# The last tile's feed-forward in a two-layer decoder kernel: h quantised by pieces and turned by TensorE inside the down product of the tile ahead

## The reference

```
def fp4_quant_dequant(x):            # blocks of 16
    scale = max(max|block| / 6, 1e-12)
    idx = searchsorted(MID, |block / scale|)
    return GRID[idx] * sign(block) * scale
def fp4_linear(x, w):  return einsum('bsk,nk->bsn', quant(x), quant(w))
h = silu(fp4_linear(x, w_gate)) * fp4_linear(x, w_up)
x = layernorm(x + fp4_linear(h, w_down))
```

## Time and profile before

| what | us |
|---|---|
| median of 3 runs | 2803.29 (2802.55 to 2804.59) |
| the profiled execution | 2801.17 |
| its span | 2799.6 |
| busy: TensorE matmul / VectorE / GpSimd / ScalarE | 2630.1 / 1907.7 / 865.4 / 808.7 |
| mean granted clock of TensorE | 0.978 of 2.4 GHz |

### The profile page before, as it was taken

How to read it: one execution, slowest core, us unless ns; L and a number is a source line. 1 busy time by engine, 2 the same in 40 slices (tenths; PEclk the granted TensorE clock), 3 DMA queues, 4 the chain that set the end, 5 groups by cost and what they waited for, 6 DMA issues and landing times. The chain is left out here.

```text
span 2799.6 us, 36866 instructions
## 1 busy us (share of the span) xinstructions
PE 2630.1 (94%) x13006; PEld 1586.6 (57%) x13006; DVE 1907.7 (68%) x3304; ACT 808.7 (29%) x1193; POOL 865.4 (31%) x902
## 2 busy tenths in 40 slices
PE   7999988999998889999998679999999999999996
PEld 3444534555555444444444346777777777777774
DVE  3688403666667336666678658888888888888884
ACT  1111312333332246666668511111111111111110
POOL 1232103554554346666667501111111111111000
PEclk9999989999999999999999989999999999999998
DMA  5344130000000133333335501111111111111111
GB/s 161 118 164 173 49 112 14 1 1 1 1 1 1 54 104 93 87 95 92 99 101 147 159 27 41 43 44 43 43 43 43 43 44 43 43 44 44 40 38 34
DMA packets 219395, 176.91 MB, mean 63 GB/s; under 512 B 38319, under 2 KB 184111, under 8 KB 218190
## 3 DMA queue, kind: packets, MB, share of 16 engines
q1 hardware_dynamic: 182230, 147.85, 17.6%
q10 hardware_dynamic: 36984, 26.71, 3.5%
HBM read 90.51 MB, written 52.43 MB: 51 GB/s over the span
## 5 line engine op out<-in xcount | busy, mean ns | idle before, releaser
L2016 PE MATMUL bank<-tiles,tl_XQT 128*128 128x512 f32 (+1 forms) x768 | 331.8, 575 | 7.6 <-DMA tl_XQT<-tl_QB 4.9
L2031 PE MATMUL bank<-tiles,tl_HT 128*128 128x512 f32 x704 | 316.3, 605 | 19.7 <-DMA tl_HT<-tl_tmp 19.7
L2021 PE MATMUL bank<-tiles,tl_XQT 128*128 128x512 f32 (+1 forms) x768 | 318.0, 557 | 0.0
L2031 PEld LDWEIGHTS bank<-tiles,tl_HT 128*128 128x128 f32 x704 | 225.2, 324 | 95.3 <-issue 28.0
L2016 PEld LDWEIGHTS bank<-tiles,tl_XQT 128*128 128x128 f32 x768 | 232.5, 310 | 74.0 <-issue 16.4
L2021 PEld LDWEIGHTS bank<-tiles,tl_XQT 128*128 128x128 f32 x768 | 236.7, 308 | 65.6 <-issue 0.2
L1376 POOL TENSOR_SCALAR_AFFINE_SELECT tiles<-tiles 128x512 f32<-128x512 f32 x256 | 179.5, 704 | 202.6 <-ACT tiles L1595 187.2
L1969 POOL TENSOR_TENSOR tl_rs<-tl_ve,mhalf 128x1 f32<-128x1 f32 x32 | 17.6, 549 | 593.0 <-DVE tl_ve L2124 593.0
L2065 ACT ACTIVATE tl_HQ<-bank 128x512 f32<-128x512 f32 (+1 forms) x96 | 53.9, 562 | 427.7 <-PE bank L2016 406.3
L1702 DVE SCALAR_TENSOR_TENSOR tiles<-tiles,bank 128x1024 f32<-128x1024 f32 (+1 forms) x128 | 141.7, 1148 | 25.2 <-PE bank L1475 25.2
L1381 POOL TENSOR_SCALAR_AFFINE_SELECT tiles<-tiles 128x512 f32<-128x512 f32 x224 | 152.6, 681 | 0.0
(11 more groups left out here) (279 smaller groups left out, 4961.1 us busy)
## 6 DMA issues: line engine op xcount, KB each, us to landing
tl_HT<-tl_tmp SPq DMA_DIRECT2D x256, 44.0 KB, 1.9
tl_HT<-tl_tmp ACTq DMA_DIRECT2D x256, 44.0 KB, 2.0
fp_weights<-space_quant ACTq DMA_DIRECT2D x33, 256.0 KB, 2.2
X<-in_x SPq DMA_DIRECT2D x8, 1024.0 KB, 12.0
v<-tiles SPq DMA_DIRECT2D x32, 256.0 KB, 2.4
unit_g<-tiles SPq DMA_DIRECT2D x32, 256.0 KB, 2.4
unit_gT<-tiles SPq DMA_DIRECT2D x32, 256.0 KB, 2.8
la_GN<-unit_g SPq DMA_DIRECT2D x128, 64.0 KB, 2.0
```

What stands on the lines that cost most here:

```text
L2016: mm = e.matmul(bank[(2 * q) % 3][:, 0:w], chunk(XQT[n % 2], c), WgT[q][:, :, c, :], start=(c == 0), stop=(c == C - 1))
L2021: mm = e.matmul(bank[(2 * q + 1) % 3][:, 0:w], chunk(XQT[n % 2], c), WuT[q][:, :, c, :], start=(c == 0), stop=(c == C - 1))
L2031: mm = e.matmul(bank[DOWN][:, :], chunk(HT, q), WdT[:, q, :], start=(q == 0), stop=(q == IC - 1))
```

## The change

For the last tile alone (`LT`, tile 31) the h path is a different one; the other 31 tiles keep theirs (`by_blocks`).

- VectorE: `last_h(q)` quantises piece q by itself, all nine steps, with `XB` in place of `tmp`. `last_h(0)` stands in slot 31 behind `h_turned(30)` and ahead of `product(31, 1)`, `last_h(1)` behind that product, `last_h(2)` behind `product(31, 2)`, where `h_divide` stood. The multiplication with the scales is done by quarters of the row (one behind piece 0, one behind piece 1, two behind piece 2) and writes into the other `HQ` buffer (`HL`) in such an order that each chunk of the down product is a run of 128 columns.
- TensorE: in `down(30)`, ahead of its ninth matmul, `last_turned` waits for all products and all four multiplications, and makes 11 transposes of 128 x 128 into banks 0, 1 and 2.
- ScalarE: `last_copied`, in slot 31 behind the last SiLU, copies the three banks into `tmp` (`HLT`), which the DMAs of tile 30 have left by then.
- TensorE: `last_down` in slot 32 multiplies from there, into bank 4, each group of four chunks behind its copy. It does not wait for `out_sum(30)`.
- Gone for tile 31: `h_divide`, `h_rounders`, `h_rounded`, `h_scaled`, `h_turned` over the whole width, and the 16 DMAs.

```
--- before.py
+++ after.py
@@ -1881,6 +1881,7 @@
         s_g, s_sg, s_u, s_h, s_hs, s_hq = (sem(n) for n in ("gate_mm", "silu", "up_mm", "h", "h_step", "hq"))
         s_ht, s_hd, s_d, s_a6, s_t6, s_m6, s_v6, s_r6, s_x6, s_out = (sem(n) for n in (
             "hq_turned", "hqT", "down_mm", "sum6", "stats6", "mean6", "var6", "rstd6", "x6", "stored"))
+        s_ls, s_lq, s_lt, s_lc = (sem(n) for n in ("last_h_step", "last_hq", "last_hqT_mm", "last_hqT"))
         XT, PT, SM = sb("XT", [P, C, P]), sb("PT", [P, P]), sb("SM", [P, HM])
         mx, sm, rc = (sb(n, [P, H]) for n in ("mx", "sm", "rc"))
         st4, mv4, ve4, rs4 = sb("st4", [P, 6]), [sb(f"mv4{p}", [P, 2]) for p in range(2)], sb("ve4", [P, 1]), sb("rs4", [P, 1])
@@ -1904,6 +1905,10 @@
         x_tile = lambda n: k.x_tile(n % B, n // B)
         rows = lambda n: slice(HM * (n % 2), HM * (n % 2) + HM)
         there = lambda n: 0 <= n < NT
+
+        LT = NT - 1
+        by_blocks = lambda n: 0 <= n < LT
+        HL, HLT = HQ[NT % 2], tmp
         SLOTS = range(-3, NT + 3)
 
         def blocks_moved(e, token_rows, src, dst, done):
@@ -1941,7 +1946,7 @@
                         n = s - 2
                         e.wait_ge(s_x6.sem, s_x6.at(n + 1))
                         e.dma_start(k.out[n % B, (n // B) * P:(n // B + 1) * P, :], x_tile(n)).then_inc(s_out.sem, 16)
-                    if there(s - 1):
+                    if by_blocks(s - 1):
                         h_moved(e, s - 1, (0, 1))
                     if there(s + 1):
                         xq_moved(e, s + 1, (0, 1))
@@ -2028,7 +2033,24 @@
                     e.wait_ge(s_a6.sem, s_a6.at(n))
                     e.wait_ge(s_hd.sem, s_hd.at(256 * (n + 1)))
                     for q in range(IC):
+                        if n == LT - 1 and q == IC - 3:
+                            last_turned()
                         mm = e.matmul(bank[DOWN][:, :], chunk(HT, q), WdT[:, q, :], start=(q == 0), stop=(q == IC - 1))
+                    mm.then_inc(s_d.sem, 1)
+
+                def last_turned():
+                    e.wait_ge(s_h.sem, s_h.at(NP * NT))
+                    e.wait_ge(s_lq.sem, s_lq.at(4))
+                    for q in range(IC):
+                        mm = e.transpose(bank[q // C][:, q % C * P:(q % C + 1) * P], HL[:, q * P:(q + 1) * P], k.ident[:, :])
+                        if q % C == C - 1 or q == IC - 1:
+                            mm.then_inc(s_lt.sem, 1)
+
+                def last_down():
+                    e.wait_ge(s_a5.sem, s_a5.at(NT))
+                    for q in range(IC):
+                        e.wait_ge(s_lc.sem, s_lc.at(q // C + 1))
+                        mm = e.matmul(bank[VOUT][:, :], HLT[:, q * P:(q + 1) * P], WdT[:, q, :], start=(q == 0), stop=(q == IC - 1))
                     mm.then_inc(s_d.sem, 1)
 
                 for s in SLOTS:
@@ -2046,8 +2068,10 @@
                         gate_and_up(s, 2)
                     if there(s + 2):
                         transpose_weights(s + 2)
-                    if there(s - 1):
+                    if by_blocks(s - 1):
                         down(s - 1)
+                    if s - 1 == LT:
+                        last_down()
                     if there(s + 2):
                         attend(s + 2)
 
@@ -2072,6 +2096,12 @@
                     e.wait_ge(s_pm.sem, s_pm.at(n + 1))
                     e.wait_ge(s_v.sem, s_v.at(n))
                     e.activation(PT[rows(n), :], bank[WEIGHTS][rows(n), 0:P], ACT.Copy).then_inc(s_pc.sem, 1)
+
+                def last_copied():
+                    e.wait_ge(s_hd.sem, s_hd.at(256 * LT))
+                    for n, (x, w) in enumerate(PIECES):
+                        e.wait_ge(s_lt.sem, s_lt.at(n + 1))
+                        e.activation(HLT[:, x:x + w], bank[n][:, 0:w], ACT.Copy).then_inc(s_lc.sem, 1)
 
                 for s in SLOTS:
                     if there(s + 2):
@@ -2082,10 +2112,12 @@
                         exp(s + 2)
                     if there(s):
                         silu(s, 1)
-                    if there(s - 1):
+                    if by_blocks(s - 1):
                         h_moved(e, s - 1, (2, 3))
                     if there(s):
                         silu(s, 2)
+                    if s == LT:
+                        last_copied()
                     if there(s + 2):
                         copy_weights(s + 2)
                     if there(s + 1):
@@ -2096,7 +2128,7 @@
                 def out_sum(n):
                     y = x_tile(n)
                     e.wait_ge(s_d.sem, s_d.at(n + 1))
-                    e.tensor_tensor(y, bank[DOWN][:, :], y, ALU.add).then_inc(s_a6.sem, 1)
+                    e.tensor_tensor(y, bank[DOWN if by_blocks(n) else VOUT][:, :], y, ALU.add).then_inc(s_a6.sem, 1)
                     e.wait_ge(s_a6.sem, s_a6.at(n + 1))
                     e.bn_stats(st6[:, :], y).then_inc(s_t6.sem, 1)
                     e.wait_ge(s_t6.sem, s_t6.at(n + 1))
@@ -2236,16 +2268,50 @@
                     e.wait_ge(s_hq.sem, s_hq.at(n + 1))
                     e.transpose(turned(tmp[:, :]), HQ[n % 2][:, :]).then_inc(s_ht.sem, 1)
 
+                def last_h(q):
+                    (x, w), n, at = PIECES[q], LT, QUANT * q
+                    part = slice(x // BLK, (x + w) // BLK)
+                    y, t, c, r = HQ[n % 2][:, x:x + w], XB[:, 0:w], sc[n % 2][:, part], rs[:, part]
+                    e.wait_ge(s_h.sem, s_h.at(NP * n + q + 1))
+                    e.wait_ge(s_hs.sem, s_hs.at(QUANT * n))
+                    e.tensor_reduce(am[:, part], blocks(y), AX.X, ALU.max, apply_absolute_value=True).then_inc(s_ls.sem, 1)
+                    e.wait_ge(s_ls.sem, s_ls.at(at + 1))
+                    e.tensor_scalar(c, am[:, part], 1.0 / 6.0, 1e-12, ALU.mult, ALU.max).then_inc(s_ls.sem, 1)
+                    e.wait_ge(s_ls.sem, s_ls.at(at + 2))
+                    e.reciprocal(r, c).then_inc(s_ls.sem, 1)
+                    e.wait_ge(s_ls.sem, s_ls.at(at + 3))
+                    e.tensor_scalar(r, r, 1.0 - 2.0 ** -23, None, ALU.mult).then_inc(s_ls.sem, 1)
+                    e.wait_ge(s_ls.sem, s_ls.at(at + 4))
+                    e.tensor_tensor(blocks(y), blocks(y), spread(r), ALU.mult).then_inc(s_ls.sem, 1)
+                    e.wait_ge(s_ls.sem, s_ls.at(at + 5))
+                    e.wait_ge(s_xs.sem, s_xs.at(QUANT * NT))
+                    e.tensor_scalar(t.bitcast(U32), y.bitcast(U32), 0x7F800000, None, ALU.bitwise_and).then_inc(s_ls.sem, 1)
+                    e.wait_ge(s_ls.sem, s_ls.at(at + 6))
+                    e.tensor_scalar(t, t, 1.0, MAGIC, ALU.max, ALU.mult).then_inc(s_ls.sem, 1)
+                    e.wait_ge(s_ls.sem, s_ls.at(at + 7))
+                    e.tensor_tensor(y, y, t, ALU.add).then_inc(s_ls.sem, 1)
+                    e.wait_ge(s_ls.sem, s_ls.at(at + 8))
+                    e.tensor_tensor(y, y, t, ALU.subtract).then_inc(s_ls.sem, 1)
+
+                    e.wait_ge(s_ls.sem, s_ls.at(at + QUANT))
+                    e.wait_ge(s_ht.sem, s_ht.at(n))
+                    for j in ((0,), (1,), (2, 3))[q]:
+                        of = lambda v: v[:, j * v.shape[1] // 4:(j + 1) * v.shape[1] // 4]
+                        by_half = lambda v: v.rearrange("p (c u k) -> p c u k", c=IC, u=2)
+                        scale = of(sc[n % 2]).rearrange("p (c u) -> p c u", u=2).unsqueeze(3).to_broadcast([P, IC, 2, BLK])
+                        e.tensor_tensor(HL[:, :].rearrange("p (c j u k) -> p j c u k", c=IC, j=4, u=2)[:, j],
+                                        by_half(of(HQ[n % 2])), scale, ALU.mult).then_inc(s_lq.sem, 1)
+
                 for s in SLOTS:
                     if there(s - 2):
                         out_sum(s - 2)
                     if there(s + 1):
                         attended_sum(s + 1)
-                    if there(s - 1):
+                    if by_blocks(s - 1):
                         h_rounders(s - 1)
                     if there(s + 1):
                         attended_normal(s + 1)
-                    if there(s - 1):
+                    if by_blocks(s - 1):
                         h_rounded(s - 1)
                     if there(s):
                         product(s, 0)
@@ -2253,13 +2319,17 @@
                         shifted(s + 2)
                     if there(s - 2):
                         out_normal(s - 2)
-                    if there(s - 1):
+                    if by_blocks(s - 1):
                         h_scaled(s - 1)
                         h_turned(s - 1)
                     if there(s + 2):
                         weights(s + 2)
+                    if s == LT:
+                        last_h(0)
                     if there(s):
                         product(s, 1)
+                    if s == LT:
+                        last_h(1)
                     if there(s + 1):
                         x_quant(s + 1)
                         xq_turned(s + 1)
@@ -2269,8 +2339,10 @@
```

(4 more changed lines are left out.)

## The result

| | us |
|---|---|
| before, median of 4 runs | 2802.92 (2802.51 to 2804.59) |
| after, median of 4 runs | 2785.15 (2784.02 to 2786.48) |
| ratio, 95% interval | 0.9936 (0.9918 to 0.9953) |
| profiled execution after, its span | 2784.02, 2782.3 |

The change made the kernel 17.8 us faster; forecast were 15.6 and a median of 2787.7, in a range that began at 2785.6. The direction and the place were right. The two pull in opposite directions, since a falling clock makes the kernel slower and not faster; the experiments take them apart.

What follows compares the result with a forecast made beforehand. A serial path in the last tile, with TensorE idle 18.38 us, was taken as the bound. TensorE ending at 2777.3 instead of 2792.93 saves 15.6 us: 2785.6, plus 2.1 for the median, 2787.7; range 2785.6 to 2791.9.

Steps and rivals of the forecast that it cites:

- VectorE's path: Quantising and scaling tile 31 by pieces on VectorE, from the end of h_turned(30) at 2746.75 to 2763.49: 16.74 us.
- TensorE up to the wait: In down(30), TensorE's first eight matmuls end at 2760.6, it stands 2.9 us for VectorE, then eleven transposes take 1.38 us.
- The three matmuls of tile 30: The last three matmuls of tile 30's down product, behind the transposes, take 2.63 us, to 2767.5.
- rival A: TensorE's clock falls around the transposes, costing 1.4 to 2.7 us, middle 2.0, for 2789.7 us; chance 35%.
- The rule on transposes: Transposes do not count as clock activity: the gap is then 4.3 us; if they counted, 2.9 us and the clock holds.
- The copies: ScalarE's copies of the transposes cost nothing, covered by tile 30's last three matmuls; without those, about 1 us.
- The last product and the tail: Tile 31's down product takes 9.81 us, to 2777.3; the end of the span behind it keeps its 6.67 us.
- nothing before that moves: Everything ahead of the end of h_turned(30), at 2746.75, keeps its time.
- the median of the runs is 2.1 us above this execution: Step from the profiled execution to the median: 2.1 us added to 2785.6 gives the forecast 2787.7 us.
- B: VectorE takes longer than its rows by the scaling's upper bound, 1.4 us, for 2789.1 us; chance 10%.
- C: Slower than before through the four scalings, 2809 us at 0.27 us a block; 5%, shared with smaller losses of most gain.
- D: VectorE done before TensorE's eighth matmul, so the 2.9 us stand goes too: 2784.8 us; small form within the forecast's 50%.

Runs made afterwards that it cites:

- filler: The changed kernel with three wide matmuls of unused result ahead of TensorE's wait for VectorE; median 2783.05 us, ratio 0.9933 to the kernel before.
- late: The changed kernel with the 11 transposes behind the eleventh matmul of tile 30, not ahead of the ninth; median 2783.54 us, ratio 0.9934 to the kernel before.
- again: The changed kernel unedited, measured a second time; median 2786.79 us, ratio 0.9943 to the kernel before.
- again2: The changed kernel unedited, measured a third time; median 2786.64 us, ratio 0.9949 to the kernel before.

## Why the prediction came out as it did

- *VectorE's path.* Forecast from the start of `h_turned(30)` to the end of the last scaling 19.44 us, measured 18.85. The scaling, the unknown of the sum, took 0.53 us against 0.526. What was too dear were the runs of steps: 5.01 us from the first reduction to the next product for 5.18 (and that reduction starts 0.14 us before the block transpose ends), 5.09 for 5.18, and 4.88 for 5.07 in the last, narrower one.
- *TensorE up to the wait.* The stand was 2.2 us for 2.9, the transposes 1.32 to the next wide matmul for 1.38. Right.
- *The three matmuls of tile 30.* "6 x 0.439 = 2.63 us" is the step whose mechanism failed: it is priced at full clock, and from the first of them to the last product it took 4.18 us, since the clock fell. This is rival A, which had 35%; its price here is 1.6 us (filler: 3.92 for 5.50 us from the first transpose on), at the lower end of the 1.4 to 2.7 given for it. The forecast called the clock's holding likelier; it fell in five of five profiles with that stand.
- *The rule on transposes* of the Trainium skill (TensorE: Matmul & The Clock Gate, "Part 4: PE-mode transpose") is not decided by these runs. The prediction had said that with transposes counted the clock would hold over a stand of 2.9 us, and it fell with one of 2.2, which speaks for the rule. But no run has such a stand without transposes behind it, or a long row of transposes without a stand; in filler and late, where 1.36 us of transposes alone lay between wide matmuls, the clock held.
- *The copies.* "Without them it would cost about 1 us" was too dear: in late, without the three matmuls, about 0.2 us of the copies shows.
- *The last product and the tail.* 9.60 for 9.81. Up to the end of the product the errors are -0.59 (VectorE), +0.15 (from its end to the first transpose), -0.06 (transposes), +1.55 (the three matmuls) and -0.21 (the last product), together 0.84: the local gain is 14.8 where 15.6 was forecast. The tail gave 0.3 that I had at nothing. What that 0.3 is, the runs do not say; kernels without the 16 DMAs in slot 32 have 6.23 to 6.32 us there, those with them 6.45 to 6.63. That 15.1 us came so near to 15.6 is luck in part: VectorE, the last product and the tail gave back 1.1 of the 1.55 that the clock took.
- *From the execution to the median.* The clock made the kernel slower than forecast, so it is not what put the median below the range. That was the stretch ahead of the edit, which the prediction put at nothing ("nothing before that moves"): in the trace of after `h_turned(30)` starts 2.2 us earlier than in that of before. Without this the median would have been 2787.3, inside the range. The second such term is "the median of the runs is 2.1 us above this execution"; for the changed kernel it was 1.1. From the forecast of 2787.7 to the measured 2785.15 the terms are +0.8 local, -0.3 tail, -2.2 ahead of the edit, -1.0 from the execution to the median, and +0.15 for what lies around the span. The terms of 2.2 and 1.0 are scatter: I took it from three runs that span 2 us, where the runs of before here span 2798.43 to 2805.4, and the start moved by 2.9 us among three profiles of the changed kernel. The first measurement's difference of 17.8 is a high draw: again and again2 gave 14.8 and 16.1, with medians of 2786.79 and 2786.64, inside the range. The lower end should have been some 2 us lower.
- Rivals B, C and D: the scalings cost what their rows said, so B and C had no ground; D's condition, VectorE done by the end of TensorE's eighth matmul, was missed by 2.2 us.

## What to carry to other kernels

Look for the stretch in which no engine is busy for long, and in it for steps that wait for all of a tile where a part would do; two cuts at different links of one serial chain can add up, if no in-order queue puts an old step in between (here the store of tile 30 ahead of SP's DMAs, 3.0 us) and if no engine's other work comes to lie in the path. Put the work that waits for another engine behind the last independent work and not amid it: here that was worth 3.8 us, 2.2 of stand and 1.6 of clock. And measure a local change by a stretch between two marks in the trace: in the changed kernel it repeated to 0.02 us, while whole executions of the kernel before were up to 7 us apart. Where the stretch holds a rise of the clock it repeats less well: the kernel before and sems, the same but for unused semaphores, are 1.65 us apart in it.

## What the runs showed of the hardware

- An unedited instruction near the end starts at times up to 5.4 us apart in 14 profiles; in the one pair that was followed, the 2.2 us go with another granted clock between 440 and 480 us. What set that clock is not shown.
- Eleven 128 x 128 transposes take 1.36 us at full clock, 2.58 at the low level. A product of 22 records behind 18.4 us of idleness took 11.14, 11.17 and 12.77 us, and 9.6 behind other work at full clock.
- With 2.2 us of stand and transposes behind it the clock fell, five profiles of five; with the stand filled, or not there, it held, three of three.
- ScalarE's copy out of PSUM into a stride of 11 floats takes 1.8 times as long as a dense one (2.66 for 1.47 us for three, one profile of strided).
